# Last tiles of a mixture-of-experts layer: four tiles summed on chip instead of three, two sums at the end, comparisons in quarters

## The chip, the cores and the metric

The kernel runs on one core of one Trainium2 chip. The metric is the device time of one execution in microseconds. TensorE is PE, VectorE DVE, ScalarE ACT, GpSimd POOL, SyncE SP (here it issues DMAs only).

## The reference

The input x is 4 x 256 tokens of 256 numbers. The result is two layers with normalisation and residuals, in f32:

```python
x = x + layernorm(attention(layernorm(x)))   # 16 heads of 128, rotary, causal
h = layernorm(x).reshape(1024, 256)
logits = h @ router_weight.T + router_bias   # 16 experts, top 4, softmax of those
for each expert e:                           # 256 -> 2 x 256 -> 256
    gate, up = (h @ gate_up[e] + bias)[..., ::2], [..., 1::2]
    out_e = (clip(up, -7, 7) + 1) * min(gate, 7) * sigmoid(1.702 * gate) @ down[e] + down_bias[e]
x = x + layernorm(sum over e of score[e] * out_e)
```

## The kernel before, in words

The first 340 us or so are the attention part, which the change leaves alone. The expert part works on tiles of 128 rows. Each token is written four times, once for each of its experts, into rows_d in DRAM, sorted by expert; a row holds the token's 256 numbers, its 16 scores and its token number (column TOKEN). TILE_MAX is 47 tiles, of which EARLY = 9 can be started before the last quarter of the tokens is routed. A table says for each tile which expert it has and where its rows begin (`entry(i, 0)`, `entry(i, 1)`).

For tile i the engines do this, each in the order written out in its own block:

- SP, `load_rows` (L443): loads the tile's 128 rows into one of XG = 9 buffers xg, once the scatter-add of tile i - 9 has landed.
- PE, `turn_tile` (L1503): transposes the rows; ACT, `xgT_out` (L759): copies them out of PSUM; DVE and ACT, both `place_gu` (L1138, L771): copy half of the expert's gate/up weights each into gu_now.
- PE, `gate_up` (L1512, matmuls L1522): 16 matmul records into bank 2 or 3. DVE, `clamp` (L1147): gate and up out of PSUM; ACT, `gelu` (L765); DVE, `gated` (L1163): their product, act.
- PE, `down` (L1527, matmuls L1536), two tiles later: into bank 4 or 5 (ps_y). ACT, `weigh` (L779): times the score, into one of YR = 5 row buffers y.
- POOL, `add_rows` (L607, L612): an indirect DMA with addition (scatter-add) of the 128 rows to the tokens' rows of a sum in DRAM. There are SUMS = 3 such sums, taken in turn, i % 3, and a scatter-add waits for the landing of the one before it on the same sum.

In the loop (L1632, L1289, L893) PE does turn_tile(i + 1), gate_up(i), down(i - 2); DVE place_gu(i + 1), clamp(i), gated(i); ACT place_gu(i + 1), xgT_out(i + 1), gelu(i), weigh(i - 2).

The last LATE = 3 tiles (LAST = 44 and on) are not scattered. ACT writes their weighted rows rounded to the fp32r format (late_h), and DVE the remainder (late_l, `late_low`, L1282), after the loop. DVE makes the 0/1 matrix turn[j] for each, `rows_to_tokens` (L1273): a cast of the token numbers, a subtraction, and one comparison of 128 x 1024 elements (L1279), behind the gated products of tiles 40, 41 and 42. PE then adds, for each of the four pairs of token tiles u, turn times late_h and late_l into a bank ps_sum[u]: `add_late` (L1640), four matmuls of 256 columns a call.

At the end SP loads the three sums from DRAM (L470 to L476) into sum_a, sum_b (halves) and sum_c (quarters), 1 MB each. POOL adds sum_b to sum_a (`add_second`, L631, in four pieces) and then sum_c (`add_third`, L638). PE adds the result to the banks by a product with the identity in f32 (`add_sums`, L1651, L1655), between the late tiles 1 and 2. For each pair u, DVE takes the statistics out of the bank (L934 to L941), POOL makes the power -0.5 (L493), DVE scales and adds x (`finish`, L1299, L1305), ACT adds the shift (`shift_result`, L904, L910), SP stores the pair (L479). All four pairs are in a chain like that.

## Time and profile before

| what | us |
|---|---|
| runs shown, median (lowest to highest) | 511.5 (510.91 to 516.53) |
| the profiled execution, its own time | 514.36 |
| its span, first to last instruction | 512.6 |
| PE busy | 469.9 (92%) |
| DVE busy | 356.6 (70%) |
| ACT busy | 325.5 (63%) |
| POOL busy | 248.5 (48%) |

The time of an execution holds a little more than the span of its instructions. Busy shares are means over the whole span; where the end is set has to be read from the timelines. In a timeline's row stand the start, the duration, engine, line, operation, tiles written and read, how many are merged (x), and in brackets how long the engine was idle before and what released it. In a row of windows stand the window, its length, the busy time and number of operations of PE, PEld (weight loads), DVE, ACT, POOL, the granted clock of TensorE (1.00 is 2.4 GHz, 0.50 is 1.2 GHz), the DMA share and GB/s.

### The profile page before, as it was taken

The page shows a single profiled execution, that of the slowest core. Times are in us where ns is not written, and L with a number is a line of the kernel's source. Part 1 is how long each engine was busy: PE and PEld are TensorE (multiplying, and loading weights), DVE is VectorE, ACT ScalarE, POOL GpSimd, SP SyncE. Part 2 cuts the span into 40 slices and gives each one's busy share as a digit, 9 for nine tenths or more (in the row PEclk, how much of TensorE's full clock was granted, in tenths as well). Part 3 has the DMA queues.
Part 4 walks back from the last instruction along what each step waited for, and adds up shares of the span by engine and source line. Part 5 has one row for each costly group of instructions (what it writes and reads, how often), then busy time and mean ns, then how long its engine had stood idle before and what let it go on. Part 6 is the DMA issues. An engine that isn't in the chain of part 4 may idle for free. (4 is left out here: it accounts for less than half of the span.)

```text
span 512.6 us, 11665 instructions
## 1 busy us (share of the span) xinstructions
PE 469.9 (92%) x3466; PEld 439.8 (86%) x3466; DVE 356.6 (70%) x1258; ACT 325.5 (63%) x815; POOL 248.5 (48%) x236
## 2 busy tenths in 40 slices
PE   6699999999999999999999999789889999999933
PEld 3698898999899999999999998588789999998833
DVE  4698788686866686876687797376666767668605
ACT  4878986768586767576676656546458665655402
POOL 1888884444222355435442245016835555554363
PEclk9999999999999999999999999998899999999967
DMA  8357651999400000000365346533655555655742
GB/s 240 108 188 234 213 182 35 374 369 370 159 1 1 22 25 36 23 26 36 127 212 179 127 140 212 165 115 67 139 104 102 93 106 92 105 91 79 160 127 84
DMA packets 63406, 67.49 MB, mean 132 GB/s; under 512 B 4529, under 2 KB 58225, under 8 KB 63345
## 3 DMA queue, kind: packets, MB, share of 16 engines
q1 hardware_dynamic: 54896, 55.79, 34.6%
q0 software_dynamic: 7872, 10.49, 11.8%
q8 instruction: 30, 0.49, 0.4%
q10 hardware_dynamic: 576, 0.46, 0.3%
q14 instruction: 32, 0.25, 0.2%
HBM read 32.63 MB, written 34.10 MB: 130 GB/s over the span
## 5 line engine op out<-in xcount | busy, mean ns | idle before, releaser
L514 POOL TENSOR_TENSOR by_sin<-by_sin,rope_sin 128x512 f32<-128x512 f32 x64 | 82.4, 1288 | 148.5 <-ACT by_sin L659 148.5
L1522 PE MATMUL bank<-xgT,gu_now 128*128 128x128 f32 x752 | 95.1, 281 | 3.6 <-ACT xgT L659 1.7
L659 ACT ACTIVATE by_sin<-bank 64x512 f32<-64x512 f32 x128 | 75.7, 592 | 34.1 <-PE bank L1324 32.6
L612 POOL DMA_INDIRECT sum_d<-y,xg x44 | 68.5, 1558 | 58.7 <-ACT y L787 55.1
L1522 PEld LDWEIGHTS bank<-xgT,gu_now 128*128 128x128 f32 x752 | 90.9, 198 | 5.0 <-DVE gu_now L1143 3.8
L681 ACT ACTIVATE prob<-score,row_bias 128x128 f32<-128x128 f32 (+1 forms) x128 | 57.1, 447 | 47.2 <-DVE row_bias L971 47.1
L1324 PE MATMUL bank<-xT_h,qk_h 128*128 128x256 f32 x256 | 77.5, 303 | 4.3 <-DVE qkT L961 1.7
L971 DVE CUSTOM_DVE_ANT_0 score<-bank,mask 128x128 f32<-128x128 f32 (+1 forms) x128 | 40.3, 351 | 52.2 <-issue 52.2
L1324 PE MATMUL bank<-xT_h,qk_l 128*128 128x256 f32 x256 | 72.2, 282 | 0.0
L1324 PE MATMUL bank<-xT_l,qk_h 128*128 128x256 f32 x256 | 72.1, 282 | 0.0
L1324 PEld LDWEIGHTS bank<-xT_h,qk_h 128*128 128x128 f32 x256 | 48.8, 191 | 5.1 <-POOL qk_l L499 3.4
L1536 PE MATMUL bank<-dn_w,act 128*128 x188 | 48.4, 382 | 1.9 <-DVE act L1169 1.2
L1324 PE MATMUL bank<-wo_h,oT_h 128*128 128x256 f32 x128 | 41.7, 326 | 9.0 <-DVE oT_l L986 8.8
L961 DVE TENSOR_TENSOR qkT<-bank,by_sin 128x512 f32<-128x512 f32 x64 | 44.2, 691 | 7.1 <-POOL by_sin L514 1.3
L1324 PEld LDWEIGHTS bank<-xT_l,qk_h 128*128 128x128 f32 x256 | 48.8, 191 | 0.0
L1324 PEld LDWEIGHTS bank<-xT_h,qk_l 128*128 128x128 f32 x256 | 48.6, 190 | 0.0
L769 ACT ACTIVATE glu<-gate 128x256 f32<-128x256 f32 x47 | 19.6, 417 | 44.2 <-DVE gate L1153 44.1
L1324 PE MATMUL bank<-wv_h,xT_h 128*128 128x256 f32 x128 | 47.5, 371 | 0.0
L953 DVE TENSOR_TENSOR bank<-bank,rope_cos 128x512 f32<-128x512 f32 x64 | 44.4, 694 | 1.2 <-ACT by_sin L659 1.2
L1153 DVE TENSOR_SCALAR gate<-bank,gate_bias 128x128 f32<-128x128 f32 x94 | 28.5, 345 | 20.7 <-PE bank L1522 20.6
L980 DVE TENSOR_SCALAR prob<-prob,row_rec 128x128 f32<-128x128 f32 (+1 forms) x128 | 40.2, 357 | 2.3
L659 ACT ACTIVATE gu_now<-gu_w 128x512 f32 x47 | 31.7, 675 | 14.1 <-issue 13.0
(182 smaller groups left out, 1178.6 us busy)
## 6 DMA issues: line engine op xcount, KB each, us to landing
rows_d<-blank SPq DMA_DIRECT2D x32, 576.0 KB, 7.5
gu_w<-_L_ffn_gate_up_proj_dram SPq DMA_DIRECT2D x16, 512.0 KB, 5.7
xg<-rows_d SPq DMA_DIRECT2D x47, 144.0 KB, 2.6
dn_w<-in_L_ffn_down_proj_dram SPq DMA_DIRECT2D x16, 256.0 KB, 3.0
sum_d<-blank SPq DMA_DIRECT2D x2, 1152.0 KB, 9.9
raw_qk<-in_L_attn_wq_dram SPq DMA_DIRECT2D x16, 128.0 KB, 3.6
raw_qk<-in_L_attn_wk_dram SPq DMA_DIRECT2D x16, 128.0 KB, 3.7
raw_v<-in_L_attn_wv_dram SPq DMA_DIRECT2D x8, 256.0 KB, 2.7
```

Source lines behind the costliest of these rows:

```text
L514: pool.tensor_tensor(v, v, rope_sin[:, :].unsqueeze(1).broadcast_to([P, 2, T]), ALU.mult).then_inc(pool_sin, 1)
L612: pool.indirect_dma_start(out=sum_d[i % SUMS], out_offset=bass.IndirectOffsetOnAxis(ap=xg[:, i % XG, TOKEN:TOKEN + 1].bitcast(U32), axis=0 ...
L659: return sc.activation(out, in_, ACT.Copy)
L681: e = sc.activation(prob[:, n % 2, lo:hi], score[:, n % 2, lo:hi], ACT.Exp, bias=row_bias[:, n % 2, i:i + 1], scale=-1.0, accum_out=row_su ...
L953: dve.tensor_tensor(v, v, rope_cos[:, :].unsqueeze(1).broadcast_to([P, 2, T]), ALU.mult).then_inc(dve_cos, 1)
L961: dve.tensor_tensor(qkT[:, n % QR, :, :].rearrange("p w t -> p (w t)"), ps_qk[n % 2][:, :], by_sin[:, n % 2, :], ALU.add).then_inc(dve_rop ...
L971: m = dve.tensor_tensor_reduce(score[:, n % 2, lo:hi], ps_s[:, lo:hi], mask[:, P:T] if i == 0 else mask[:, :], -1.0 / D, FILL, ALU.add, AL ...
L980: m = dve.tensor_scalar(prob[:, n % 2, lo:hi], prob[:, n % 2, lo:hi], row_rec[:, n % 2, i:i + 1], None, ALU.mult)
L1153: m = dve.tensor_scalar(gate[:, i % 2, r, :], ps_gu[i % 2][:, r * P:(r + 1) * P], gate_bias[:, bass.ds(e * 2 + r, 1)], LIMIT, ALU.add, ALU ...
L1324: m = pe.matmul(out, lhs, rhs, start=first and i == 0, stop=last and i == len(terms) - 1, skip_group_check=not (first and last))
L1522: m = pe.matmul(ps_gu[i % 2][:, (2 * s + r) * P:(2 * s + r + 1) * P], gu_now[:, i % 2, k, s, r * P:(r + 1) * P], xgT[:, i % XT, k, :], sta ...
L1536: m = pe.matmul(ps_y[i % 2][:, 0:M], act[:, i % AR, r, :], dn_w[:, bass.ds(e, 1), r, :].rearrange("p o m -> p (o m)"), start=(r == 0), sto ...
```

## The change

- YR goes from 5 to 4, LATE from 3 to 4, so LAST is 43. The scatter-adds are those of tiles 0 to 42.
- HOME says which sum each tile goes to: in turn over three up to tile 37, and the last five (38 to 42) in turn over two, so that one sum is whole after tile 37. SP loads it into sum_a then, in the loop; the other two (of tiles 41 and 42) into sum_b and sum_c, both in quarters.
- The token numbers of the late tiles come by four small loads of their own (late_token, 128 x 2 numbers each), behind the rows of tile 17. DVE casts and subtracts for all four tiles at once behind tile 19 (`token_rows`), and each comparison is cut into four of 128 x 256, one behind each of tiles 20 to 35 (`which_token`).
- late_low of tiles 43 and 44 stands in the loop, behind the gated products of tiles 45 and 46. The down product of tile 46 goes into the gate/up bank of tile 45 (ps_out) and waits for that tile's clamp only.
- POOL's additions are gone. DVE adds sum_b to sum_a (`add_two`). PE does all products of the first three late tiles, and then for each pair those of the fourth, the identity product of sum_a and that of sum_c.
- The last pair's result is stored in two halves, the second by ACT's own queue.

```diff
@@ -39,7 +39,7 @@
 BLANK = E * REGION
-XG, XT, AR, YR, SUMS, LATE = 9, 2, 3, 5, 3, 3
+XG, XT, AR, YR, SUMS, LATE = 9, 2, 3, 4, 3, 4
 FILL_STEP = 4
@@ -177,6 +177,7 @@
         late_l = sb("late_l", [P, LATE, M], F32R)
+        late_token = sb("late_token", [P, LATE, 2], I32)
         token = sb("token", [P, LATE])
@@ -201,6 +202,7 @@
         ps_y = bank[4:6]
+        ps_out = [ps_y[i % 2] for i in range(TILE_MAX - 1)] + [ps_gu[TILE_MAX % 2]]
         ps_sum = bank[6:8] + bank[0:2]
@@ -343,7 +346,12 @@
         LAST = TILE_MAX - LATE
-        ENDING = [(LAST + k) % SUMS for k in range(SUMS)]
+        TWO = LAST - 5
+        HOME = [i % SUMS if i < TWO else (TWO + (i - TWO) % 2) % SUMS for i in range(LAST)]
+        def added(i):
+            return 16 * HOME[:i + 1].count(HOME[i])
@@ -444,7 +452,7 @@
                 if i >= XG:
-                    sp.wait_ge(dma_sum[(i - XG) % SUMS], 16 * ((i - XG) // SUMS + 1))
+                    sp.wait_ge(dma_sum[HOME[i - XG]], added(i - XG))
                 sp.dma_start(xg[:, i % XG, :], rows_d[bass.ds(row, P), :]).then_inc(dma_xg[i % XG], 16)
@@ -464,20 +472,27 @@
             start_sum(3)
-            for i in range(EARLY + 3, TILE_MAX):
+            for i in range(EARLY + 3, EARLY + XG):
                 load_rows(i)
-            for i, to, signal in ((ENDING[0], sum_a, dma_first), (ENDING[1], sum_b, dma_second)):
-                sp.wait_ge(dma_sum[i], 16 * ((LAST - 1 - i) // SUMS + 1))
-                for u in range(2):
-                    sp.dma_start(to[:, 4 * u:4 * u + 4, :], sum_rows[i][:, 4 * u:4 * u + 4, :]).then_inc(signal[u], 16)
-            sp.wait_ge(dma_sum[ENDING[2]], 16 * ((LAST - 1 - ENDING[2]) // SUMS + 1))
-            for u in range(4):
-                sp.dma_start(sum_c[:, 2 * u:2 * u + 2, :], sum_rows[ENDING[2]][:, 2 * u:2 * u + 2, :]).then_inc(dma_third[u], 16)
-            for u in range(4):
+            for j in range(LATE):
+                row = sp.value_load(entry(LAST + j, 1), min_val=0, max_val=BLANK)
+                sp.dma_start(late_token[:, j, :], rows_d[bass.ds(row, P), TOKEN:TOKEN + 2].bitcast(I32)).then_inc(dma_token, 16)
+            for i in range(EARLY + XG, TILE_MAX):
+                load_rows(i)
+            sp.wait_ge(dma_sum[HOME[TWO - 1]], added(TWO - 1))
+            for u in range(2):
+                sp.dma_start(sum_a[:, 4 * u:4 * u + 4, :], sum_rows[HOME[TWO - 1]][:, 4 * u:4 * u + 4, :]).then_inc(dma_first[u], 16)
+            for i, to, signal in ((LAST - 2, sum_b, dma_second), (LAST - 1, sum_c, dma_third)):
+                sp.wait_ge(dma_sum[HOME[i]], added(i))
+                for u in range(4):
+                    sp.dma_start(to[:, 2 * u:2 * u + 2, :], sum_rows[HOME[i]][:, 2 * u:2 * u + 2, :]).then_inc(signal[u], 16)
+            for u in range(3):
                 sp.wait_ge(act_moe, 2 * u + 2)
                 sp.dma_start(out_rows[:, 2 * u:2 * u + 2, :], sum_b[:, 2 * u:2 * u + 2, :]).then_inc(dma_out, 16)
-            sp.wait_ge(dma_out, 16 * 4)
+            sp.wait_ge(act_moe, TILES - 1)
+            sp.dma_start(out_rows[:, TILES - 2, :], sum_b[:, TILES - 2, :]).then_inc(dma_out, 16)
+            sp.wait_ge(dma_out, 16 * 5)
@@ -608,10 +623,10 @@
                 if i >= SUMS:
-                    pool.wait_ge(dma_sum[i % SUMS], 16 * (i // SUMS))
-                pool.indirect_dma_start(out=sum_d[i % SUMS], out_offset=bass.IndirectOffsetOnAxis(
+                    pool.wait_ge(dma_sum[HOME[i]], added(i) - 16)
+                pool.indirect_dma_start(out=sum_d[HOME[i]], out_offset=bass.IndirectOffsetOnAxis(
                     ap=xg[:, i % XG, TOKEN:TOKEN + 1].bitcast(U32), axis=0), in_=y[:, i % YR, :], in_offset=None,
-                    compute_op=ALU.add).then_inc(dma_sum[i % SUMS], 16)
+                    compute_op=ALU.add).then_inc(dma_sum[HOME[i]], 16)
@@ -628,28 +643,7 @@
-            def add_second(u):
-                pool.wait_ge(dma_first[u // 2], 16)
-                pool.wait_ge(dma_second[u // 2], 16)
-                tiles = slice(2 * u, 2 * u + 2)
-                pool.tensor_tensor(sum_a[:, tiles, :], sum_a[:, tiles, :], sum_b[:, tiles, :], ALU.add).then_inc(pool_first, 1)
-            def add_third(u):
-                pool.wait_ge(dma_third[u], 16)
-                pool.wait_ge(pool_first, u + 1)
-                tiles = slice(2 * u, 2 * u + 2)
-                pool.tensor_tensor(sum_a[:, tiles, :], sum_a[:, tiles, :], sum_c[:, tiles, :], ALU.add).then_inc(pool_whole, 1)
             for u in range(4):
-                add_second(u)
-            add_third(0)
-            add_third(1)
-            add_third(2)
-            power("moe", 0)
-            add_third(3)
-            for u in range(1, 4):
                 power("moe", u)
@@ -779,12 +773,12 @@
                 if i >= LAST:
-                    sc.activation(late_h[:, i - LAST, :], ps_y[i % 2][:, 0:M], ACT.Copy,
+                    sc.activation(late_h[:, i - LAST, :], ps_out[i][:, 0:M], ACT.Copy,
                                   scale=xg[:, i % XG, bass.ds(e + M, 1)]).then_inc(act_y, 1)
...
                 if i >= YR:
-                    sc.wait_ge(dma_sum[(i - YR) % SUMS], 16 * ((i - YR) // SUMS + 1))
-                sc.activation(y[:, i % YR, :], ps_y[i % 2][:, 0:M], ACT.Copy,
+                    sc.wait_ge(dma_sum[HOME[i - YR]], added(i - YR))
+                sc.activation(y[:, i % YR, :], ps_out[i][:, 0:M], ACT.Copy,
                               scale=xg[:, i % XG, bass.ds(e + M, 1)]).then_inc(act_y, 1)
@@ -912,6 +906,8 @@
                 shift_result(u)
+            sc.wait_ge(act_moe, TILES)
+            sc.dma_start(out_rows[:, TILES - 1, :], sum_b[:, TILES - 1, :]).then_inc(dma_out, 16)
@@ -1270,20 +1266,26 @@
             experts[EARLY] = place_gu(EARLY)
-            def rows_to_tokens(j):
-                i = LAST + j
-                dve.wait_ge(dma_xg[i % XG], 16 * (i // XG + 1))
-                chain(dve.tensor_copy(token[:, j:j + 1], xg[:, i % XG, TOKEN:TOKEN + 1].bitcast(I32)))
-                chain(dve.tensor_scalar(from_end[:, j, :], full_edge[:, :], token[:, j:j + 1], None, ALU.subtract))
-                dve.tensor_tensor(turn[:, j, :, :], from_end[:, j, :].unsqueeze(2).broadcast_to([P, TILES, P]),
-                                  countdown[:, :].unsqueeze(1).broadcast_to([P, TILES, P]), ALU.is_equal).then_inc(dve_turn, 1)
+            def token_rows():
+                dve.wait_ge(dma_token, 16 * LATE)
+                dve.tensor_copy(token[:, :], late_token[:, :, 0]).then_inc(dve_token, 1)
+                dve.wait_ge(dve_token, 1)
+                dve.tensor_tensor(from_end[:, :, :], full_edge[:, :].unsqueeze(1).broadcast_to([P, LATE, TILES]),
+                                  token[:, :].unsqueeze(2).broadcast_to([P, LATE, TILES]), ALU.subtract).then_inc(dve_token, 1)
+                dve.wait_ge(dve_token, 2)
+            def which_token(j, u):
+                tiles = slice(2 * u, 2 * u + 2)
+                dve.tensor_tensor(turn[:, j, tiles, :], from_end[:, j, tiles].unsqueeze(2).broadcast_to([P, 2, P]),
+                                  countdown[:, :].unsqueeze(1).broadcast_to([P, 2, P]), ALU.is_equal).then_inc(dve_turn, 1)
...
                 dve.wait_ge(act_y, i + 1)
-                dve.scalar_tensor_tensor(out=late_l[:, j, :], in0=ps_y[i % 2][:, 0:M], scalar=xg[:, i % XG, bass.ds(e + M, 1)],
+                dve.scalar_tensor_tensor(out=late_l[:, j, :], in0=ps_out[i][:, 0:M], scalar=xg[:, i % XG, bass.ds(e + M, 1)],
                                          in1=late_h[:, j, :].bitcast(F32), op0=ALU.mult, op1=ALU.subtract).then_inc(dve_late, 1)
@@ -1291,10 +1293,24 @@
                 gated(i)
-                if LAST - 4 <= i < LAST - 4 + LATE:
-                    rows_to_tokens(i - LAST + 4)
-            for j in range(LATE):
+                if i == EARLY + 10:
+                    token_rows()
+                if EARLY + 10 < i <= EARLY + 10 + 4 * LATE:
+                    which_token((i - EARLY - 11) // 4, (i - EARLY - 11) % 4)
+                if i - 2 >= LAST:
+                    late_low(i - 2 - LAST, experts[i - 2])
+            for j in range(LATE - 2, LATE):
                 late_low(j, experts[LAST + j])
+            def add_two(u):
+                dve.wait_ge(dma_first[u // 2], 16)
+                dve.wait_ge(dma_second[u], 16)
+                tiles = slice(2 * u, 2 * u + 2)
+                dve.tensor_tensor(sum_a[:, tiles, :], sum_a[:, tiles, :], sum_b[:, tiles, :], ALU.add).then_inc(dve_two, 1)
+            for u in range(4):
+                add_two(u)
@@ -1528,12 +1544,14 @@
                 pe.wait_ge(dve_act, i + 1)
-                if i >= 2:
+                if i == TILE_MAX - 1:
+                    pe.wait_ge(dve_up, i)
+                elif i >= 2:
                     pe.wait_ge(act_y, i - 1)
-                if i - 2 >= LAST:
-                    pe.wait_ge(dve_late, i - 1 - LAST)
+                    if i - 2 >= LAST:
+                        pe.wait_ge(dve_late, i - 1 - LAST)
                 for r in range(2):
-                    m = pe.matmul(ps_y[i % 2][:, 0:M], act[:, i % AR, r, :],
+                    m = pe.matmul(ps_out[i][:, 0:M], act[:, i % AR, r, :],
                                   dn_w[:, bass.ds(e, 1), r, :].rearrange("p o m -> p (o m)"),
@@ -1637,31 +1655,32 @@
-            def add_late(u, j, first=False, last=False):
-                pe.wait_ge(dve_turn, j + 1)
+            def add_late(u, j, first=False):
+                pe.wait_ge(dve_turn, 4 * j + u + 1)
                 pe.wait_ge(dve_late, j + 1)
...
                     for rows in (late_h, late_l):
-                        m = pe.matmul(ps_sum[u][:, s * M:(s + 1) * M], turn[:, j, 2 * u + s, :], rows[:, j, :],
-                                      start=first and s == 0 and rows is late_h, stop=last and s == 1 and rows is late_l,
-                                      skip_group_check=True)
+                        pe.matmul(ps_sum[u][:, s * M:(s + 1) * M], turn[:, j, 2 * u + s, :], rows[:, j, :],
+                                  start=first and s == 0 and rows is late_h, stop=False, skip_group_check=True)
+            def add_sum(u, rows, last=False):
+                for s in range(2):
+                    m = pe.matmul(ps_sum[u][:, s * M:(s + 1) * M], ident[:, :], rows[:, 2 * u + s, :], start=False,
+                                  stop=last and s == 1, skip_group_check=True)
                 return m
-            def add_sums(u):
-                pe.wait_ge(pool_whole, u + 1)
-                for s in range(2):
-                    pe.matmul(ps_sum[u][:, s * M:(s + 1) * M], ident[:, :], sum_a[:, 2 * u + s, :], start=False, stop=False,
-                              skip_group_check=True)
             pe.wait_ge(act_xgT, TILE_MAX)
+            for j in range(LATE - 1):
+                for u in range(4):
+                    add_late(u, j, first=j == 0)
             for u in range(4):
-                add_late(u, 0, first=True)
-            for u in range(4):
-                add_late(u, 1)
-                add_sums(u)
-                add_late(u, 2, last=True).then_inc(pe_sum, 1)
+                add_late(u, LATE - 1)
+                pe.wait_ge(dve_two, u + 1)
+                add_sum(u, sum_a)
+                pe.wait_ge(dma_third[u], 16)
+                add_sum(u, sum_c, last=True).then_inc(pe_sum, 1)
...
 # ---- launch: one core; inputs and outputs as the reference has them ----
```

## Rows read from the trace of the kernel before

**Rows 1.** Windows of the core: busy us of each engine, granted clock, DMA share, GB/s
```profile
378.00:440.00 62.00, 62.00 (x480) 58.80 (x479) 43.16 (x131) 40.55 (x96) 33.43 (x22) 1.00 0.56 96
484.00:487.30 3.30, 3.30 (x24) 3.08 (x24) 0.89 (x2) 0.47 (x1) 0.00 (x0) 1.00 1.08 275
...
495.00:498.00 3.00, 2.80 (x9) 2.44 (x10) 0.00 (x0) 0.00 (x0) 2.59 (x3) 0.50 0.00 0
```

**Rows 2.** PE's timeline: start, us, engine, line, operation, tiles, [idle before <-releaser]
```profile
455.37 1.95 PE L1522 MATMUL bank<-xgT,gu_now 128*128 128x128 f32 x16
...
463.98 1.95 PE L1522 MATMUL bank<-xgT,gu_now 128*128 128x128 f32 x16
...
476.82 1.95 PE L1522 MATMUL bank<-xgT,gu_now 128*128 128x128 f32 x16
...
483.88 1.13 PE L1536 MATMUL bank<-dn_w,act 128*128 x4 [0.73 <-ACT late_h L782]
...
484.96 0.28 PE L1646 MATMUL bank<-late_l,turn 128*128 128x256 f32 x1
...
487.11 0.28 PE L1646 MATMUL bank<-late_l,turn 128*128 128x256 f32 x1
495.20 2.07 PE L1655 MATMUL bank<-sum_a,ident 128*128 128x256 f32 x4 [7.82 <-POOL sum_a L643]
...
501.22 1.02 PE L1655 MATMUL bank<-sum_a,ident 128*128 128x256 f32 x4
...
503.03 1.03 PE L1655 MATMUL bank<-sum_a,ident 128*128 128x256 f32 x4
```

**Rows 3.** The chain that ended last, in order of time: start, us, what
```profile
482.08 6.80 DMA sum_b<-sum_d
```

**Rows 4.** POOL's timeline over the last tiles and the sums
```profile
464.91 1.55 POOL L612 DMA_INDIRECT sum_d<-y,xg  x1 [1.32 <-ACT y L787]
...
480.80 1.57 POOL L612 DMA_INDIRECT sum_d<-y,xg  x1 [1.51 <-ACT y L787]
489.02 4.91 POOL L636 TENSOR_TENSOR sum_a<-sum_a,sum_b 128x512 f32<-128x512 f32 x4 [6.65 <-DMA sum_b<-sum_d]
```

**Rows 5.** DVE's timeline in the tile loop, a tile without and one with comparisons
```profile
459.48 0.43 DVE L1143 COPY gu_now<-gu_w 128x512 f32 x1 [0.37 <-issue]
...
464.81 0.15 DVE L1277 CAST token<-xg 128x1 f32<-128x1 int32 x1
...
465.27 1.23 DVE L1279 TENSOR_TENSOR turn<-from_end,countdown 128x1024 fp32r<-128x1024 f32 x1
466.41 0.42 DVE L1143 COPY gu_now<-gu_w 128x512 f32 x1
```

**Rows 6.** Landings of L612 (min/median/max) and loads and stores: KB each, median us to landing
```profile
DMA to landing us min/median/max: 3.7/4.3/6.9
...
sum_a<-sum_d SPq DMA_DIRECT2D x2, 512.0 KB, 5.1
...
sum_c<-sum_d SPq DMA_DIRECT2D x4, 256.0 KB, 3.9
out_dram<-sum_b SPq DMA_DIRECT2D x4, 256.0 KB, 2.2
...
rope_cos<-in_rope_cos_dram ACTq DMA_DIRECT2D x1, 128.0 KB, 3.3
```

**Rows 7.** The row buffers early in the experts: SP's load of tile 11, ACT's row write
```profile
367.63 0.34 SPq L448 DMA_DIRECT2D xg<-rows_d  x1
...
368.35 0.46 ACT L787 ACTIVATE y<-bank,xg 128x256 f32<-128x256 f32 x1
```

**Rows 8.** Early DVE operation on two tiles of SBUF, 512 columns, min/median/max ns
```profile
L1132 DVE TENSOR_TENSOR wv_l<-raw_v,wv_h x1: 1781/1781/1781, 11.2 to 11.2; 128x512 fp32r<-128x512 f32 x1
```

**Rows 9.** DVE's timeline of the last statistics
```profile
498.17 0.76 DVE L934 BATCH_NORM_STATS2 stats<-bank 128x6 f32<-128x256 f32 x2 [11.93 <-PE bank L1646]
...
505.12 0.75 DVE L934 BATCH_NORM_STATS2 stats<-bank 128x6 f32<-128x256 f32 x2
```

7 lines of the change are left out of this document (4 added, 3 removed).

## The prediction

> **What bounds the kernel now.** I read the windows first, then the timelines of the single engines over the last 60 us, then the chain. From 378 to 440 us PE is busy for all 62 us at full clock [rows 1]: the tile loop is PE's, with 22 matmul records to a tile. Gate_up of tiles 38 and 41 begin at 455.37 and 463.98, so a tile takes 8.61 / 3 = 2.87 us. DVE and ACT have gaps in it: of DVE's, one is 0.37 us ahead of the copy into gu_now [rows 5]. POOL issues one scatter-add a tile, 1.55 us of it, and waits for ACT's row write between them [rows 4].
>
> The end is different. The last matmul that needs nothing from the sums starts at 487.11; the next starts at 495.20, after 7.82 us of idle [rows 2]. The chain runs through the landing of tile 42's scatter-add and then the first half of the load of sum_b, 6.80 us [rows 3], to POOL, which adds sum_b to sum_a in four pieces, 4.91 us from 489.02 [rows 4], and then sum_c. PE comes back at half its clock: 1.00 in the window up to 487.3, 0.50 from 495 to 498 [rows 1]. The first statistics of the result start at 498.17, the last at 505.12 [rows 9], and what follows them is a fixed tail. So the time is set by (a) when PE ends the tiles, (b) what lies between there and the first statistics, (c) the pace of the four pairs of tiles.
>
> **The sum, in three steps.** First, *the tile loop's end*. Gate_up of tile 41 starts at 463.98 and of tile 45 at 476.82: 12.84 us for four tiles that at 2.87 us would need 11.48 [rows 2]. The excess, 1.36 us, is where the three comparisons of 1024 columns (1.23 us each, 465.27 the first) push the copy of gu_now to 466.41 with no gap before it [rows 5]; they stand behind the gated products of tiles 40 to 42. The change cuts each into quarters, one behind each of 16 tiles from tile 20 on. A comparison occupies DVE from 465.27 to 466.41, 1.14 us for 1024 columns, so a quarter costs some 0.29 us plus what is fixed; I take 0.34, bounds 0.29 and 1.14. The cover: each old set had two small operations ahead of it, 1.60 us in all from 464.81 to 466.41, 0.46 of it ahead of the comparison [rows 5]. Three sets are 4.8 us of DVE work and cost PE 1.36 us, so about 1.15 us a tile were hidden; I use 1.0. A quarter fits three times over: cost nothing, gain 1.36 us. If that cover were gone, it would be 16 x 0.34 = 5.4 us. The token work moves to tile 19, two small operations (0.46 us were spent on two such before), covered too; its data are loaded some ten tiles earlier.
>
> Then the end of the loop itself. Before, PE had nothing from 483.15 until down(46) at 483.88, because that waited for ACT's late_h and DVE's late_l to empty its bank [rows 2]. Down(46) now writes a gate/up bank that has been free since tile 45's clamp, so it follows the gated product: 483.15 - 1.36, plus 0.15 because this product is itself just ready, is 481.95. From 483.88 to the second late product at 484.96 were 1.08 us, less one spacing of 0.12 us 0.96; so the late products begin near 482.9.
>
> Second, *from there to the first statistics*. A late product is 256 columns: eighteen spacings from 484.96 to 487.11 make 0.12 us each [rows 2]. The change does 3 x 4 x 4 = 48 of them, and 4 of tile 46, before the first sum: 52 x 0.12 = 6.24 us, to 489.1. Then two pairs of plain f32 products with the identity, sum_a (which DVE has added) and sum_c. Their price: between 501.22 and 503.03 lie one pair of them and eight late products, 1.81 - 8 x 0.12 = 0.85 us a pair. Two pairs are 1.7 us: 490.8. The statistics begin about 0.2 us after that, 491.0 to 491.1, against 498.17: 7.1 us earlier. PE has no gap on this way, so I price it at full clock.
>
> Is everything else there by then? DVE ends tile 46's late_l near 484 (ACT has to write late_h after down(46), which ends at 482.8). Its four additions of 512 columns: the nearest rows are 1.23 us for 1024 columns on DVE [rows 5] and 4.91 / 4 = 1.23 us for the same addition on POOL [rows 4]; I take 0.65, so they end at 486.6, at POOL's price at 489. Either is early enough for 490. The loads: tile 42 now is the last scatter-add. At the loop's pace it starts at 464.91 + 4 x 2.87 = 476.39, against 480.80 for tile 43 before [rows 4]. Landing takes 4.3 us in the median and 6.9 at most [rows 6], so sum_c is asked for at 480.7 to 483.3, lands a quarter 3.9 us later [rows 6] (and a little more for the later ones): 484.6 to 487.2 for the first. It is needed at 489.1 + 0.85 = 490.0. sum_b follows tile 41, 473.52 + 4.3 = 477.8, and at sum_a's 5.1 us [rows 6] is there at 483. What was POOL's 4.91 us and half of what the loads took is gone from the path; what is late next is PE's own stream.
>
> Third, *the pace of the pairs*. After the first, PE needs 4 x 0.12 + 2 x 0.85 = 2.2 us a pair of tiles. Before, the four statistics took 505.12 - 498.17 = 6.95 us [rows 9], with one stretched pair at half clock. DVE's own work for a pair (statistics and scaled addition) is of the same size, so 3 x 2.2 = 6.6 us: another 0.35 us. The tail after the last statistics is unchanged but for the stores: the last pair goes out as two halves, the second from ACT's queue. A 256 KB store lands in 2.2 us, and 128 KB on ACT's queue took 3.3 us at the kernel's start [rows 6]; so between 0.5 us better and 1.1 us worse. I take nothing.
>
> Sum: 7.1 + 0.35 = 7.4 us off the span of 512.6, to 505.2. The profiled execution took 514.36, which would be 507.0. The median of the runs shown is 511.5, and on it the forecast is 504.1.
>
> **Edits that cost nothing.** One row buffer less: ACT's row write of tile i now waits for the scatter-add of i-4. In the loop that is 4 x 2.87 = 11.5 us against 6.9 at worst. Early it is tight: tile 6's row write at 368.35 now needs tile 2's scatter-add, which had landed by 367.63, since SP's load of tile 11 waited for just that [rows 7]; 0.7 us are left, and ACT has slack behind it. If it failed, a few tenths. Two alternating sums for the last five scatter-adds: each waits for the one two tiles back, 5.74 us against 4.3, and 6.9 at worst; a wait on POOL then delays the scatter-adds behind it, nothing else. Four token loads on SP, ahead of tile 18's rows: each about an issue of 0.34 us [rows 7] and a register load; the rows behind them have a lead of several tiles. late_l inside the loop stands behind the gated product of tiles 45 and 46, in DVE's gaps.
>
> A rule that speaks against the quarters: POOL makes its descriptors while DVE compares. The only row of contention is an early subtraction, 1.78 us for 512 columns beside a POOL operation of the same kind [rows 8], while 1024 columns of comparison took 1.23 us at 465.27 beside POOL's scatter-add of 464.91 [rows 4, 5]. The Trainium skill, "GPSIMD Engine Reference", section "1. Specifications", says that GpSimd shares its SBUF interfaces with VectorE, with contention for DVE instructions that have two SBUF inputs. The comparison has two. By that rule a quarter would be stretched as the subtraction was, per column some 2.9 times, to about 1 us, and would just fill the cover. The rows speak against it here; it is part of why the third rival keeps its chance.
>
> **The rivals.** *The loads still set the end* (chance 0.12). sum_a's load, now in the loop, slows tile 39's scatter-add to the 6.9 us seen; tile 41's then starts at 467.78 + 6.9 = 474.7, lands at 481.6, and sum_b takes 6.80 us [rows 3] to 488.4, with sum_c's quarters of 1.7 us behind it. The first arrives at 490.1 and the last at 495.2; PE waits for each, and a slow half more makes it up to 2 us. Gain 5.6 us: 505.9. For it: the long landings seen were those beside the loads. Against: these figures stack the worst cases.
>
> *PE at half clock* (0.05, the slower side). All of the tail now hangs on PE: 52 products and four pairs, 6.24 + 4 x 2.2 = 15 us of it at full clock. At half clock the first statistics come 4.7 us (twice the late products) and 1.7 us later, and each pair takes 4.4 us: 491.1 + 6.4 + 3 x 4.4 = 510.7 for the last statistics against 505.12, 5.5 us slower than before, 517.0. It decides from the point at which 7.4 of the 15 us run at half clock. For it: the 0.50 in the window from 495 [rows 1]. Against: that came behind 7.82 us of idle, and the late products ahead of it ran at 1.00. The Trainium skill, "TensorE: Matmul & The Clock Gate", section "Loop structure matters more than you think", has the same picture: long waits between matmuls bring the half clock, dense work keeps the full one. By that rule this rival has no cause here.
>
> *The quarters are not covered* (0.08): PE loses up to 5.4 us over 16 tiles, the gain is 2.0 us: 509.5. Against it: the cover of 1 us. *The change doesn't do what it says* (0.07), a wait I priced at nothing, such as the two alternating sums or the token loads, takes the place of the old one: within 1% of before, about 510.
>
> **How the numbers follow.** My own case has 0.68, and its range is 502.5 to 505.7 (stores, the price of a pair, the additions). A 1% step is 5.1 us, about what a measurement of this kernel can tell from no change. Faster by over 1% holds my case and most of the first rival: 0.78. Within 1%: the third and fourth and the rest of the first, 0.17. Slower: 0.05. The range to hold 8 in 10 reaches from 501.3 (a pair at 2.0 us and the stores better, with runs a little below the median) to 508.5, which takes in the first rival and stops short of the uncovered quarters.
>
> **What would show it.** Gate_up keeps 2.87 us a tile up to tile 45, with a 256-column comparison of about 0.43 us behind each of 16 tiles and no PE wait for gu_now. PE's idle of 7.82 us is gone; 64 late products run at 0.12 us with the clock at 1.00 up to the last pair; the first statistics start near 491, the last near 497.7. The chain names PE's identity products, and no POOL addition. It would be wrong if PE waited for sum_c or for DVE's addition, if the clock fell before the last pair, or if DVE's copy of gu_now held gate_up in the middle of the loop.

## The result, and the profile after

The kernel before takes 512.46 us in the median of 19 runs (509.13 to 516.53), the changed one 508.25 us (505.97 to 512.98, 19 runs). The ratio is 0.9936, 95% interval 0.9913 to 0.9959: 3.3 us faster, where 7.4 us were forecast. (The ratio leaves out runs far above the fastest of their kernel, here some of before; the medians are 4.2 us apart.) 508.25 is inside the range of 501.3 to 508.5, at its very end, and outside the 502.5 to 505.7 of the case that was thought likeliest; by the ratio, the gain is less than half of the one forecast. The profiled execution of the changed kernel took 507.35 us with a span of 505.5.

The windows of the changed kernel, with the columns of [rows 1]:

```profile
378.00:440.00 62.00, 62.00 (x476) 58.67 (x476) 47.35 (x144) 40.00 (x94) 36.00 (x22) 1.00 0.57 95
...
482.00:488.00 6.00, 6.00 (x51) 5.97 (x51) 3.00 (x6) 0.47 (x1) 0.00 (x0) 1.00 0.61 206
488.00:495.00 7.00, 7.00 (x41) 6.38 (x40) 3.62 (x16) 0.48 (x2) 1.79 (x4) 1.00 0.01 2
```

PE is busy and at full clock from the tile loop to the last pair, but for 0.21 us ahead of down of tile 46 (below); the windows that showed 0.50 before [rows 1] are gone. PE's timeline, against [rows 2]:

```profile
463.06 1.95 PE L1538 MATMUL bank<-xgT,gu_now 128*128 128x128 f32 x16
...
474.54 1.95 PE L1538 MATMUL bank<-xgT,gu_now 128*128 128x128 f32 x16
...
477.19 1.95 PE L1538 MATMUL bank<-xgT,gu_now 128*128 128x128 f32 x16
...
481.07 1.13 PE L1554 MATMUL bank<-dn_w,act 128*128 x4 [0.21 <-DVE act L1165]
...
482.16 0.28 PE L1664 MATMUL bank<-late_l,turn 128*128 128x256 f32 x1
...
488.15 0.28 PE L1664 MATMUL bank<-late_l,turn 128*128 128x256 f32 x1
488.27 1.02 PE L1670 MATMUL bank<-sum_a,ident 128*128 128x256 f32 x4
...
490.46 1.03 PE L1670 MATMUL bank<-sum_a,ident 128*128 128x256 f32 x4
...
494.87 1.02 PE L1670 MATMUL bank<-sum_a,ident 128*128 128x256 f32 x4
```

Tile 41's gate_up begins at 463.06, tile 45's at 474.54: 11.48 us, the 2.87 us a tile of the undisturbed loop. Down of tile 46 starts at 481.07, the late products run at 0.12 us from there to 488.15, and the identity products follow at once: the idle of 7.82 us is gone. DVE beside the loop and at the end, against [rows 5] and [rows 9]:

```profile
426.18 0.43 DVE L1165 SCALAR_TENSOR_TENSOR act<-up,glu 128x256 f32<-128x256 f32 x1
426.52 0.42 DVE L1281 TENSOR_TENSOR turn<-from_end,countdown 128x256 fp32r<-128x256 f32 x1
427.03 0.43 DVE L1139 COPY gu_now<-gu_w 128x512 f32 x1
```

```profile
483.35 2.49 DVE L1310 TENSOR_TENSOR sum_a<-sum_a,sum_b 128x512 f32<-128x512 f32 x4
490.19 0.76 DVE L930 BATCH_NORM_STATS2 stats<-bank 128x6 f32<-128x256 f32 x2 [4.35 <-PE bank L1670]
...
496.79 0.76 DVE L930 BATCH_NORM_STATS2 stats<-bank 128x6 f32<-128x256 f32 x2 [0.17 <-PE bank L1670]
```

The quarter of a comparison takes 0.42 us and the copy of gu_now behind it begins at 427.03, in time. The four additions of sum_b are done at 485.8, long before 488.27, and the first and the last statistics start at 490.19 and 496.79.

POOL (against [rows 4]) and SP:

```profile
473.94 1.55 POOL L627 DMA_INDIRECT sum_d<-y,xg  x1 [2.67 <-DMA sum_d<-y,xg]
475.79 1.55 POOL L627 DMA_INDIRECT sum_d<-y,xg  x1 [0.30 <-issue]
```

```profile
466.64 0.98 SPq L485 DMA_DIRECT2D sum_a<-sum_d  x2
477.73 1.92 SPq L489 DMA_DIRECT2D sum_b<-sum_d  x4
479.69 2.00 SPq L489 DMA_DIRECT2D sum_c<-sum_d  x4
```

Tile 41's scatter-add waited 2.67 us for the landing of tile 39's, as the two alternating sums can make it, and tile 42's follows at once. It cost PE nothing: sum_b is asked for at 477.73 and sum_c at 479.69, and PE waits for neither.

What is new is at the very end. Two rows of the end of the program (L51), first of the kernel before, then of the changed one: POOL's closing drain, and SP's branch after the landing of the last store.

```profile
L51 POOLq DRAIN  x1: 5143/5143/5143, 507.2 to 507.2; - x1
...
L51 SPq COMPARE_BRANCH  x1: 38/38/38, 511.2 to 511.2; - x1
```

```profile
L51 POOLq DRAIN  x1: 6450/6450/6450, 498.9 to 498.9; - x1
...
L51 SPq COMPARE_BRANCH  x1: 38/38/38, 502.8 to 502.8; - x1
```

In the changed kernel the last store has landed by 502.8 and the span ends at 505.5; before, these were 511.2 and 512.6. POOL's drain starts beside its last operation (498.9) and takes 6.45 us, to 505.3; before it took 5.14 us from 507.2, to 512.3. Both times the program ends 0.2 us behind it.

### The profile page after: what moved, and what is told of

The parts are those of the page before. It is cut to its first block and busy times, and to the rows that moved or that the text cites. A ratio compares the mean times of both kernels' runs of the same rounds, so it can differ in the third digit from the quotient of the medians.

```text
span 505.5 us, 11761 instructions
## 1 busy us (share of the span) xinstructions
PE 470.3 (93%) x3498; PEld 441.1 (87%) x3498; DVE 361.3 (71%) x1272; ACT 326.1 (65%) x815; POOL 239.8 (47%) x227
## 5 line engine op out<-in xcount | busy, mean ns | idle before, releaser
L1538 PE MATMUL bank<-xgT,gu_now 128*128 128x128 f32 x752 | 93.4, 279 | 2.7 <-ACT xgT L653 1.3
L1538 PEld LDWEIGHTS bank<-xgT,gu_now 128*128 128x128 f32 x752 | 89.3, 195 | 3.5 <-DVE gu_now L1139 2.3
L982 DVE TENSOR_TENSOR oT_l<-bank,oT_h 128x256 fp32r<-128x256 f32 x64 | 27.2, 425 | 17.6 <-ACT oT_h L653 17.5
```

Of the source, the lines that this page charges most:

```text
L1538: m = pe.matmul(ps_gu[i % 2][:, (2 * s + r) * P:(2 * s + r + 1) * P], gu_now[:, i % 2, k, s, r * P:(r + 1) * P], xgT[:, i % XT, k, :], sta ...
```

## A measure that repeats

Executions of one kernel differ by several us, more than a single part is worth. In all traces below, the time is split at the start of tile 11's gate_up, from where the loop runs undisturbed. Columns in us, with the end of the span known to 0.1: from there to tile 41's gate_up it is 86.12 or 86.13 in all traces; "loop end" is from gate_up of tile 41 to that of 46; "to stats" from there to the first statistics; "pairs" from the first to the last; "end" from there to the end of the span; "behind 11" the whole, with the 86.13.

| kernel | tile 11 at | loop end | to stats | pairs | end | behind 11 |
|---|---|---|---|---|---|---|
| before (first trace) | 377.86 | 15.49 | 18.70 | 6.95 | 7.48 | 134.74 |
| before, six more traces | 374.48 to 385.12 | 15.48 to 15.59 | 16.93 to 18.73 | 6.56 to 7.55 | 7.39 to 7.46 | 132.92 to 134.37 |
| changed (four traces) | 376.93 to 381.19 | 14.13 to 14.14 | 13.00 | 6.60 | 8.71 to 8.75 | 128.57 to 128.62 |
| last store whole, by SP | 377.93 | 14.13 | 13.00 | 6.60 | 8.71 | 128.57 |
| before, comparisons in quarters alone | 378.75 | 14.14 | 18.31 | 6.47 | 7.41 | 132.45 |
| before, PE kept busy | 383.50 | 15.49 | 17.23 | 6.58 | 7.47 | 132.90 |
| changed, POOL adds sum_b | 384.80 | 14.13 | 13.00 | 6.60 | 8.74 | 128.60 |
| changed, one more scatter-add | 383.05 | 14.14 | 12.99 | 6.60 | 7.40 | 127.25 |
| changed, three late tiles | 385.91 | 14.14 | 12.01 | 6.60 | 7.42 | 126.29 |
| changed, DVE adds sum_c too | 384.73 | 14.13 | 12.14 | 5.21 | 8.76 | 126.37 |
| three late tiles and DVE adds both (two traces) | 385.45, 386.18 | 14.13, 14.14 | 12.14, 12.64 | 5.04 | 7.41, 7.48 | 124.85, 125.42 |

The seven traces of before have a mean of 133.85 behind tile 11, so the change is worth 5.25 us there. The changed kernel repeats to 0.05 us, since nothing of its end waits for a load or a scatter-add; before's varies by 1.8 us, mostly with its loads: from gate_up 46 to the first identity product, which waits for them, its seven traces have 13.96 to 15.77 us.

## The experiments

**The two kernels again.** No edit.

> The kernel before, unchanged, for a second trace. Its two medians so far and its profiled execution do not agree (514.36 against 512.46). Theory A (the tail of before varies, because its idle PE comes back at half clock at different points and its loads land at different times): the time from tile 45's gate_up to the first statistics, 21.35 us in the first trace, differs from that by 1 us or more in a faster execution. Theory B (the variation is ahead of the tail, in the stretch up to tile 10): that time stays within 0.5 us and the gate_up of tile 38 begins earlier than 455.37 instead, by as much as the execution is faster.

> The changed kernel, unchanged, for a second trace. Both theories: from tile 45's gate_up (474.54) to the first statistics (490.19) again 15.6 us within 0.3, since no idle PE and no load lies on that way. Theory A: its times scatter less than those of the kernel before in the same call. Theory B: they scatter as much.

Ratio of before to itself 1.0002 (0.9966 to 1.0038), of the changed kernel 0.9938 (0.9902 to 0.9973). The traced execution of before was a slower one (517.16 us against 514.36), not the faster one that both theories speak of. Both hold in part: before's way from gate_up 45 to the statistics was 20.3 us instead of 21.35, and tile 11 began at 381.07 instead of 377.86. The changed kernel's way from gate_up 45 was 15.66 us (15.65 in the first trace), and its times scatter nearly as much as those of before (505.09 to 512.70 against 508.67 to 517.16). The first trace, on which the forecast was built, had one of the longest ends of the seven.

**The last store back to one, by SP.**

```diff
-            for u in range(3):
+            for u in range(4):
                 sp.wait_ge(act_moe, 2 * u + 2)
...
-            sp.wait_ge(act_moe, TILES - 1)
-            sp.dma_start(out_rows[:, TILES - 2, :], sum_b[:, TILES - 2, :]).then_inc(dma_out, 16)
-            sp.wait_ge(dma_out, 16 * 5)
+            sp.wait_ge(dma_out, 16 * 4)
...
-            sc.wait_ge(act_moe, TILES)
-            sc.dma_start(out_rows[:, TILES - 1, :], sum_b[:, TILES - 1, :]).then_inc(dma_out, 16)
```

> Only the last store goes back: the last pair is stored whole by SP, nothing by ACT's queue. In the traces the time from the last statistics' start to the end of the span is 7.5 us before and 8.7 us after. Theory C (the store on ACT's queue costs the program's end 1.2 us): 7.5 us again, and the time about 1.2 us (0.2%) under the changed kernel's. Theory D (halves are worth it, the 1.2 us is something else, such as a wait for PE at the end of the program): 8.7 to 9.0 us, and the time the same or slightly above.

8.71 us again, ratio 0.9939 (0.9907 to 0.9971). Theory C falls: the store's queue has no part in the longer end. Halving the store gained nothing either, because the end waits for POOL's drain, not for the store: whole, it has landed by 503.9, and the drain ends at 506.3.

**Comparisons in quarters alone**, on the kernel before: late_token, its loads behind tile 17's rows, token_rows and which_token as in the change, with LATE = 3.

```diff
-                if LAST - 4 <= i < LAST - 4 + LATE:
-                    rows_to_tokens(i - LAST + 4)
+                if i == EARLY + 10:
+                    token_rows()
+                if EARLY + 10 < i <= EARLY + 10 + 4 * LATE:
+                    which_token((i - EARLY - 11) // 4, (i - EARLY - 11) % 4)
```

> The kernel before with the comparisons alone changed: token numbers by three small loads of their own, 12 comparisons of 128 x 256 behind tiles 20 to 31. If the step of the sum holds: gate_up of tiles 38 to 45 at 2.87 us each (20.1 us in all against 21.45), and the end 1.3 us sooner, ratio to before 0.997. If the quarters are not covered: up to 12 x 0.34 = 4 us slower than that.

The loop's end takes 14.14 us instead of 15.49: 1.35 us off, as worked out. In the time it doesn't show: ratio 1.0012 (0.9974 to 1.0049), an interval of 3.8 us, too wide for a step of 1.35 us. What was forecast, 0.997, lies at its edge; "Where the rest goes" comes back to that.

**Who adds, and POOL's drain.** Two edits on the changed kernel, the second a scatter-add of zeros that nothing needs. In the first, the block of the same name is gone from DVE's part (not shown).

```diff
+            def add_two(u):
+                pool.wait_ge(dma_first[u // 2], 16)
+                pool.wait_ge(dma_second[u], 16)
+                tiles = slice(2 * u, 2 * u + 2)
+                pool.tensor_tensor(sum_a[:, tiles, :], sum_a[:, tiles, :], sum_b[:, tiles, :], ALU.add).then_inc(dve_two, 1)
+            for u in range(4):
+                add_two(u)
             for u in range(4):
                 power("moe", u)
```

> The changed kernel with one part back: POOL adds sum_b to sum_a, not DVE. POOL's closing drain, which the program's end waits for, took 5.14 us in the three traces of kernels that let POOL do additions after its last scatter-add, and 6.45 us in the three that don't. Theory X (it is long where POOL had nothing but small operations since its scatter-adds): 5.14 us here, and the program ends 1.3 us sooner than the changed kernel after the last statistics, unless the additions make PE wait: four of 1.25 us from about 483.4 end at 488.4, and PE needs the first at 488.3, so no wait. Theory Y (it hangs on the number of scatter-adds, 44 or 43): 6.45 us again.

```diff
             for i in range(EARLY, LAST):
                 add_rows(i)
+            pool.indirect_dma_start(out=sum_d[HOME[TWO - 1]], out_offset=bass.IndirectOffsetOnAxis(
+                ap=blank[:, TOKEN:TOKEN + 1].bitcast(U32), axis=0), in_=blank[:, 0:M], in_offset=None,
+                compute_op=ALU.add).then_inc(dma_extra, 16)
```

> The changed kernel with one more scatter-add at POOL's end, zeros onto the spare rows of a sum that no one loads: 44 in all, as in the kernel before. It needs nothing and nothing waits for it. Theory Y (POOL's closing drain hangs on the number of scatter-adds): the drain takes 5.14 us instead of 6.45, and the end comes 1.3 us sooner, 127.3 us behind tile 11's gate_up. If the drain hangs on the fourth late tile in another way: 6.45 us and 128.6.

POOL's drain in the first, in the second, and in the kernel with three late tiles below (44 scatter-adds, no addition on POOL):

```profile
L51 POOLq DRAIN  x1: 6452/6452/6452, 506.7 to 506.7; - x1
```

```profile
L51 POOLq DRAIN  x1: 5143/5143/5143, 505.0 to 505.0; - x1
```

```profile
L51 POOLq DRAIN  x1: 5145/5145/5145, 506.8 to 506.8; - x1
```

X falls and Y stands: with 44 scatter-adds the drain takes 5.14 us, with 43 it takes 6.45, whether or not POOL adds. A scatter-add that does no work makes the span behind tile 11 1.35 us shorter. In the ratios (0.9893, 0.9856 to 0.993, against 0.9888 for the changed kernel beside the same runs of before) such a step can't be told. With POOL adding sum_b the first statistics still come 13.00 us after gate_up 46 (ratio 0.9892, 0.9844 to 0.9939): moving that addition to DVE brought nothing by itself. Of the rest of the change (sum_a loaded early, the second addition as a product on PE, the order of the late products) no run shows how much each brought.

**Three late tiles.**

```diff
-XG, XT, AR, YR, SUMS, LATE = 9, 2, 3, 4, 3, 4
+XG, XT, AR, YR, SUMS, LATE = 9, 2, 3, 4, 3, 3
```

> The changed kernel with LATE back at 3 (44 scatter-adds, three late tiles, 12 quarters); all else as changed. PE has 16 late products less, 1.9 us, and needs the first quarter of sum_c 1.9 us sooner, near 487.3 in the changed kernel's trace; but tile 43's scatter-add starts 2.9 us after tile 42's, so sum_c's first quarter lands near 487 to 490. Theory M (the gain is from taking POOL and its waits off the end, and the fourth late tile adds little): within 1 us of the changed kernel, first statistics 13.0 us after tile 46's gate_up or sooner. Theory N (the fourth tile is what makes the loads early enough): PE waits for sum_c by 1 to 3 us, the first statistics later than 13.0. For the drain: X says 6.45 us, Y says 5.14.

Ratio 0.9821 (0.9772 to 0.9871), where the kernel before took 520.09 us. PE's timeline:

```profile
495.32 1.02 PE L1670 MATMUL bank<-sum_a,ident 128*128 128x256 f32 x4
497.01 1.13 PE L1670 MATMUL bank<-sum_c,ident 128*128 128x256 f32 x4 [0.67 <-DMA sum_c<-sum_d]
```

PE does wait for sum_c's first quarter, 0.67 us, but has 1.9 us less to do before it. M stands, and more: the fourth late tile costs 1 us at the first statistics and 1.3 us at the drain.

**DVE adds sum_c too.**

```diff
+            def add_three(u):
+                dve.wait_ge(dma_third[u], 16)
+                dve.wait_ge(dve_two, u + 1)
+                tiles = slice(2 * u, 2 * u + 2)
+                dve.tensor_tensor(sum_a[:, tiles, :], sum_a[:, tiles, :], sum_c[:, tiles, :], ALU.add).then_inc(dve_three, 1)
...
-                pe.wait_ge(dve_two, u + 1)
-                add_sum(u, sum_a)
-                pe.wait_ge(dma_third[u], 16)
-                add_sum(u, sum_c, last=True).then_inc(pe_sum, 1)
+                pe.wait_ge(dve_three, u + 1)
+                add_sum(u, sum_a, last=True).then_inc(pe_sum, 1)
```

> The changed kernel, but DVE adds sum_c as well, in the 4.35 us in which it waits for PE, and PE does one identity product of two tiles a pair instead of two. If PE's stream is the end (my account): first statistics 0.86 us sooner (12.1 us after tile 46's gate_up instead of 13.0), and from first to last statistics 6.6 us becomes DVE's own pace of about 6.0; together 1.4 us (0.3%) under the changed kernel. If the loads of sum_c are the end: no gain, PE waits for DVE.

```profile
491.15 2.49 DVE L1311 TENSOR_TENSOR sum_a<-sum_a,sum_b 128x512 f32<-128x512 f32 x4
493.56 2.49 DVE L1318 TENSOR_TENSOR sum_a<-sum_a,sum_c 128x512 f32<-128x512 f32 x4
497.13 0.76 DVE L931 BATCH_NORM_STATS2 stats<-bank 128x6 f32<-128x256 f32 x2 [1.08 <-PE bank L1680]
```

All eight additions fit ahead of the first statistics. PE's stream is the end, as said: 12.14 us, and then DVE's own pace, 5.21 us for the pairs, faster than expected. 2.2 us off; ratio 0.986 (0.9809 to 0.9911).

**Both together.** The two edits above.

> The changed kernel with LATE back at 3 and with DVE adding sum_c too. Alone, the first gave 126.3 us behind tile 11's gate_up and the second 126.4, against 128.6. With LATE 3 the first statistics were held by sum_c's first quarter (12.01 us after tile 46's gate_up), and a DVE addition of 0.63 us now stands between that landing and PE's product: 11.8 to 12.4 us. First to last statistics 5.2 us as with the second alone, unless the quarters of sum_c set the pace; drain 5.14. Sum: 124.9 us, within 0.7. Ratio to before 0.975 to 0.985.

> Three late tiles and both additions on DVE, a second time: 124.85 us behind tile 11's gate_up, within 0.3, against 133.8 and 128.6. Its ratio to the kernel before was 0.984 in a call in which that took 519.7 us in the mean; if the changed kernel's smaller ratio (0.994) under other conditions is an effect ahead of tile 11 of about 1.4 us, this kernel shows 0.985 to 0.988 where the kernel before takes about 512 us.

124.85 and 125.42 us behind tile 11; ratios 0.9843 (0.9811 to 0.9876) and 0.984 (0.98 to 0.988), with the kernel before at 519.28 and 520.0 us. The second trace is 0.57 us above the first, where 0.3 was allowed: its DVE waits 0.65 us for sum_b and 0.28 us for sum_c, and PE 1.35 us for DVE (0.24, 0.18 and 0.67 us in the first), so the loads bear on the end again. Beside the first of these ratios the changed kernel had 0.9888 (0.9853 to 0.9922). By the traces this version is 3.2 to 3.7 us ahead of the changed kernel. It was never timed where the kernel before takes 512 us.

**The clock.** PE kept busy in before's wait, with products that are no part of the result.

```diff
                 add_late(u, 1)
+                if u == 0:
+                    keep_busy(turn[:, 0, 0, :], late_h[:, 0, :], 64, bank[2])
                 add_sums(u)
```

> The kernel before with 64 products of 0.12 us into an unused bank in PE's wait of 7.8 us, so that its clock stays up. They are no part of the result. If the half clock in the tail is a part of what the change gains: from tile 46's gate_up to the first statistics 16.4 to 17.4 us instead of 17.65 to 18.7, from first to last 6.5 instead of 6.95, the end 1.3 to 1.8 us sooner. If the clock is no part: the same as before.

```profile
492.88 7.84 PE L1495 MATMUL bank<-late_h,turn 128*128 128x256 f32 x64
500.71 1.13 PE L1655 MATMUL bank<-sum_a,ident 128*128 128x256 f32 x4
...
502.35 0.76 DVE L934 BATCH_NORM_STATS2 stats<-bank 128x6 f32<-128x256 f32 x2 [10.46 <-PE bank L1646]
```

The pair of identity products and what follows runs at full clock. From the first identity product to the first statistics it is 1.64 us; in the first trace of before it was 2.97 us at half clock [rows 2, 9], and 2.96 or 2.97 in the six others. So 1.3 us of before's end is the clock, and the rest of the gain is the wait itself. The whole doesn't show it as well: 132.90 us are left behind tile 11 against a mean of 133.85 (and a lowest of 132.92), 0.95 us less where 1.3 to 1.8 were expected, because here the sum was ready 0.66 us later behind gate_up 46 than in the mean of before; and the ratio, 0.9979 (0.9947 to 1.0011), does not tell the two kernels apart.

**Where the rest goes.** More of both kernels, unchanged.

> The changed kernel, unchanged, a third time, beside the others of this call. Behind tile 11's gate_up everything has repeated to 0.05 us in three traces (128.6 us to the end of the span): 128.6 again. Its ratio to the kernel before: 0.989 if the whole time behind tile 11 (134.7 and 133.6 in two traces of before) counts, 0.993 to 0.994 if, as in the first result, something ahead of tile 11 takes part of it back.

> The kernel before, a third trace, for what lies behind tile 11's gate_up: 134.7 and 133.6 so far. If its tail varies more than that (a fast tail would explain why the measured gain is smaller than that of the traces): below 133. If not: 133.5 to 134.8.

> The kernel before, for the time from tile 11's gate_up to the end: 134.7, 133.6 and 133.6 so far, mean 134.0. If the smaller gain of the first measurement (3.3 to 4.3 us against 5.4 in the traces) comes from a tail of before that is often shorter than the traces had it, this and the next two have a mean of 133 or less. If the tail is not the cause, they lie between 133.4 and 134.8, and what is left lies ahead of tile 11.

> As the fourth: 133.4 to 134.8 if the tail is not the cause of the smaller gain, about 133 or less if it is. Ahead of tile 11 the traces of one chip should differ by 2 to 4 us with TensorE at half clock in one or the other stretch between 340 and 380 us.

> As the fourth and the fifth: 133.4 to 134.8 us from tile 11's gate_up to the end if the tail of before is not the cause, about 133 or less if it is.

> The kernel before, a seventh trace: 132.9 to 134.7 us behind tile 11's gate_up in six so far, mean 133.8. A value under 132.5 would say that its tail is shorter in many executions than the mean has it; a value inside that range leaves the smaller measured gain to the stretch ahead of tile 11.

> The changed kernel, a fourth time, for the ratio under this call's conditions: 128.6 us behind tile 11's gate_up. If the gain that is measured hangs on the conditions ahead of tile 11, its ratio is near 0.989 where the kernel before takes about 519 us, and near 0.994 where it takes about 512 us.

Behind tile 11 before took 133.58, 134.37, 132.92, 133.73 and 133.99 us. The third of these is as the other theory had it, the mean of all seven is 133.85: its end is not the cause. The changed kernel's ratio was 0.9888 (0.9853 to 0.9922) where before took 519.28 us in the median, and 0.9942 (0.9914 to 0.997) where it took 511.57. What differs is ahead of tile 11. Windows there of one execution of the kernel before (tile 11 at 374.48) and of one with three late tiles (385.45):

```profile
360.00:370.00 10.00, 8.68 (x58) 7.12 (x57) 6.00 (x19) 5.63 (x14) 8.17 (x7) 1.00 0.53 114
370.00:380.00 10.00, 10.00 (x81) 9.54 (x80) 6.89 (x22) 4.94 (x12) 6.09 (x5) 1.00 0.90 167
```

```profile
360.00:370.00 10.00, 7.24 (x29) 5.19 (x27) 1.79 (x6) 1.94 (x4) 8.12 (x7) 0.70 0.40 94
370.00:385.00 15.00, 11.52 (x66) 10.62 (x66) 7.94 (x25) 6.96 (x16) 4.64 (x3) 0.74 0.62 132
```

The first is at 1.00 throughout, the other at 0.70 and 0.74. Taking the spans of the timed runs less the time behind tile 11 (133.85 and 128.6), over the runs that the ratios use, tile 11 begins in the mean at 376.2 before and at 378.4 in the changed kernel beside the median of 512.47 us (28 and 11 runs), at 376.3 and 378.9 beside that of 511.57 (17 and 12), but at 383.8 and 382.9 beside that of 519.28 (11 and 6). So where the ratio is small the changed kernel comes 2.2 to 2.6 us later to tile 11, and in the third case it doesn't.

One part of the change reaches into that stretch: four row buffers instead of five. ACT's row write of tile 6 now waits for the landing of tile 2's scatter-add, and that of tile 7 for tile 3's. In two of the eleven traces with four buffers it does wait, in the first and the fourth of the changed kernel, both taken where before took about 512 us; in none of the nine traces with five buffers does it. The first trace of the changed kernel, and then the trace of before at 374.48:

```profile
366.42 0.48 ACT L781 ACTIVATE y<-bank,xg 128x256 f32<-128x256 f32 x1 [1.82 <-DMA sum_d<-y,xg]
...
368.21 0.48 ACT L781 ACTIVATE y<-bank,xg 128x256 f32<-128x256 f32 x1 [0.97 <-DMA sum_d<-y,xg]
...
370.38 3.62 PE L1538 MATMUL bank<-xgT,gu_now 128*128 128x128 f32 x16 [1.35 <-ACT xgT L653]
```

```profile
365.13 0.46 ACT L787 ACTIVATE y<-bank,xg 128x256 f32<-128x256 f32 x1
...
369.53 2.02 PE L1522 MATMUL bank<-xgT,gu_now 128*128 128x128 f32 x16
```

ACT works in order, so its copies of tile 9's rows and weights come late, PE waits for them (1.35 us, 2.16 in the fourth trace), and PE's clock is at half from 370.3 to 373.7 (372.0 to 378.9 in the fourth). Up to gate_up of tile 8 the three traces take the same time from tile 0's, 30.81 to 30.83 us. From there to tile 11 the one of before needs 9.76 us, the two of the changed kernel 12.84 and 15.24. In the traces where tile 11 comes at 381 us or later ACT gets to these rows later, at 369 us and on, and nothing waits.

So the wait is real, and it comes where the gain is missing. How much of the 2.2 to 2.6 us it makes in the mean is open: no run gave the changed kernel its fifth buffer back. The kernel before with the comparisons in quarters alone has five, and by the same sum it too came late to tile 11, at 378.5 (12 runs) against 376.2; its trace shows no such wait. Either that is scatter, or something that it shares with the changed kernel counts too.

## Why the prediction was wrong in size

*The tile loop's end*: right. 1.36 us forecast, 1.37 measured against the mean of before (1.35 against its first trace), and the quarters are covered. The bank for tile 46 freed down(46) as said: 481.07, 3.88 us behind gate_up 46, against 3.84 forecast.

*To the first statistics*: right for the changed kernel. From gate_up 46 (forecast at 479.47 - 1.36) to 491.05 were 12.94 us; measured 13.00, in four traces. The 0.12 us a late product, 0.85 us a pair and PE as the end all hold. The other side of the difference was a single execution: 18.70 us before, where seven traces have a mean of 17.90. That is 0.8 us too much gain.

*The pairs*: right, 6.6 us forecast and measured; before's mean is 6.89, so 0.3 us.

*The tail*: this step failed. It said: "The tail after the last statistics is unchanged but for the stores", and took nothing, with bounds that came from the stores alone. It is 1.3 us longer, 8.73 against 7.43. What ends the program is POOL's drain, which no row of mine showed and which I had not looked for, because the chain ended on ACT.

So behind tile 11 the sum would have had to be 1.37 + 4.90 + 0.29 - 1.30 = 5.26 us. That is what the traces show, and it would be a ratio of 0.9897. Two ratios fit it (0.9888; 0.9892 with POOL adding), and the first result and two more of the changed kernel (0.9936, 0.9938, 0.9942) are 2.0 to 2.3 us short of it, ahead of tile 11.

*One row buffer less*: this step failed as well. It stood among the edits that cost nothing: "0.7 us are left, and ACT has slack behind it. If it failed, a few tenths". The 0.7 us were read from one execution, with PE at half clock on the way to tile 8. In two of four traces of the changed kernel the row writes of tiles 6 and 7 waited 1.82 and 0.97 us, 1.90 and 1.37 us, ACT had no slack behind them, and PE came to tile 11 with 3.1 and 5.5 us more behind tile 8 than in a trace of before that was the same up to there. That is large enough for the missing 2.0 to 2.3 us; the share that it has in them stays open.

*The rivals.* The loads did not set the end, though tile 41's scatter-add did wait; the half clock did not come; the quarters were covered. The fourth, a wait priced at nothing that takes the place of the old one, came in part, at two places that it did not name: POOL's drain with 1.3 us and the row buffers, and not with all of the gain. In the rival at half clock a sum is off: the late products alone would take 6.24 us more at twice their price, not 4.7; the forecast does not hang on it. Of the rule on shared SBUF interfaces in the Trainium skill, "GPSIMD Engine Reference", section "1. Specifications": the comparison was not stretched (0.417 to 0.420 us in sixteen), but POOL's scatter-add beside it took 1.70 us instead of 1.55, each time with a comparison that had begun 0.05 to 0.14 us ahead of it. In the kernel before, where three comparisons of 1.23 us begin 0.3 us or more behind the start of a scatter-add, these took 1.54 to 1.55. That points to contention that POOL pays when it comes second; no run took the two apart.

## What to carry to other kernels

Look at what ends the program, the drains and the last semaphores of every engine, before a tail is called unchanged; the chain of work can stop short of it. A single execution of before is one draw: where its end waits for loads, take several traces and compare from a point behind the scatter. The same goes for a buffer that is taken away: what it has to spare has to be read from the executions that get there fastest, not from one that was slowed on the way. And when an end has been moved onto one engine, count whether the work that freed the old bound (here a fourth late tile, a second identity product) is still worth its own time on the new one.

## What was not expected of the hardware

- POOL's drain at the end of the program took 5.14 us in all kernels with 44 scatter-adds and 6.45 us in all with 43, to 0.01 us. Only these two counts were tried, so whether it is the count as such or what is left over of some group is open.
- POOL's instruction for a scatter-add took 1.70 us where a comparison of 0.42 us on DVE had begun just before it, against 1.55 without: the sixteen scatter-adds from 406.76 to 449.63 are all at 1.70 to 1.79, those around them at 1.54 or 1.55.
- Nearly the same code ahead of tile 11 brought its gate_up at 374.5 to 386.2 us in 20 traces, with stretches of half clock at different places between 327 and 379 us; that is more than the whole gain. Already the seven traces of before reach from 374.5 to 385.1.
